# First layer two pairs ahead of the second instead of one, in an audio tower on one Trainium2 core

## The reference, cut to what matters

```
h = tok(x)                                    # batch norm over all 64 x 252 positions
h = h + softmax_attention(layernorm(h))       # layer 0: 8 heads of 16, band of 0.1 in the scores
h = h + moe(layernorm(h))                     # 8 experts, hidden 256, exact gelu, top 2
h = h + linear_attention(layernorm(h))        # layer 1: elu features, cumulative sums, 8 x 64 values
h = h + causal_ffn(layernorm(h))              # 2 causal heads of 64, then 8 experts, hidden 512, tanh gelu
```

## Time and profile before

| | us |
|---|---|
| median of three runs | 3990.13 |
| lowest, highest | 3986.05, 3990.76 |
| the profiled execution, its own time | 3990.81 |
| its span in the profile | 3989.1 |
| TensorE busy | 3827.6 |
| VectorE busy | 3155.2 |
| ScalarE busy | 2855.2 |
| GpSimd busy | 2782.1 |

### The profile page before, as it was taken

How to read it: one execution, slowest core, us unless ns; L and a number is a source line. 1 busy time by engine, 2 the same in 40 slices (tenths; PEclk the granted TensorE clock), 3 DMA queues, 4 the chain that set the end, 5 groups by cost and what they waited for, 6 DMA issues and landing times.

```text
span 3989.1 us, 105187 instructions
## 1 busy us (share of the span) xinstructions
PE 3827.6 (96%) x41541; PEld 2742.8 (69%) x41541; DVE 3155.2 (79%) x8623; ACT 2855.2 (72%) x4958; POOL 2782.1 (70%) x2725
## 2 busy tenths in 40 slices
PE   9899999999999999999999999999999999999988
PEld 4356767777667777776777777677777767777766
DVE  4367888887888778888878788878878887888876
ACT  4257777777777777777777777777777777777764
POOL 2156777777767777776777777777777677777766
PEclk9999999999999999999999999999999999999999
DMA  6111110011111001111000111100111110011100
GB/s 181 55 30 30 33 33 17 22 30 30 33 33 32 18 20 33 30 33 33 26 24 20 30 33 33 33 17 23 29 30 33 33 33 18 20 33 30 30 17 7
DMA packets 137277, 127.71 MB, mean 32 GB/s; under 512 B 29008, under 2 KB 135568, under 8 KB 136784
## 3 DMA queue, kind: packets, MB, share of 16 engines
q1 hardware_dynamic: 136784, 120.97, 10.5%
HBM read 71.12 MB, written 49.55 MB: 30 GB/s over the span
## 4 chain that ended last, share of the span: by engine, by line
PE 71%; DVE 16%; ACT 6%; POOL 3%; issue 2%; DMA 1%; SPq 1%; ACTq 0%; DVEq 0%
PE pf L1358 12%; PE pf L1360 11%; PE pf L1359 11%; PE pa L1653 5%; DVE h L1342 4%; PE pa L1358 4%; PE pa L1359 4%; PE pa L1360 4%; PE pa L1503 3%; PE pa L1635 3%; DVE hid_hi L1328 3%; PE pa L1489 2%; ACT hid L935 2%; PE pa L1404 2%; PE pa L1465 2%
## 5 line engine op out<-in xcount | busy, mean ns | idle before, releaser
L724 POOL TENSOR_TENSOR hid_lo<-hid,hid_hi 128x504 f16<-128x504 f32 x1536 | 1805.5, 1192 | 822.5 <-DVE hid_hi L1328 822.5
L935 ACT ACTIVATE hid<-pf,vec 128x504 f32<-128x504 f32 x1536 | 1021.1, 680 | 447.9 <-PE pf L1360 407.2
L1358 PE MATMUL pf<-w_hi,hid_hi 128*126 128x128 f16 x6144 | 1127.4, 224 | 88.0 <-DVE h L1342 79.0
L1360 PE MATMUL pf<-w_hi,hid_lo 128*126 128x128 f16 x6144 | 1108.7, 221 | 0.0
L1359 PE MATMUL pf<-w_lo,hid_hi 128*126 128x128 f16 x6144 | 1108.5, 221 | 0.0
L1358 PEld LDWEIGHTS pf<-w_hi,hid_hi 128*126 128x126 f16 x6144 | 843.4, 137 | 239.5 <-DVE h L1342 161.2
L1359 PEld LDWEIGHTS pf<-w_lo,hid_hi 128*126 128x126 f16 x6144 | 845.1, 138 | 14.0 <-issue 0.2
L1360 PEld LDWEIGHTS pf<-w_hi,hid_lo 128*126 128x126 f16 x6144 | 846.8, 138 | 0.0
L1328 DVE CAST hid_hi<-hid 128x504 f16<-128x504 f32 x1536 | 765.6, 521 | 95.7 <-ACT hid L935 89.4
L1342 DVE SCALAR_TENSOR_TENSOR h<-pf,gates,h 126x128 f32<-126x128 f32 x2048 | 573.5, 342 | 144.7 <-PE pf L1360 141.7
L1358 PE MATMUL pf<-xf_hi,w_hi 128*128 128x504 f16 x1536 | 578.7, 377 | 16.9 <-ACT hid L935 16.1
(11 more groups left out here) (239 smaller groups left out, 7731.5 us busy)
## 6 DMA issues: line engine op xcount, KB each, us to landing
qk_spread<-terms SPq DMA_DIRECT2D x224, 126.0 KB, 2.6
qk_spread<-terms SPq DMA_DIRECT2D x192, 63.0 KB, 2.3
y_scratch<-hid SPq DMA_DIRECT2D x32, 252.0 KB, 2.1
y_in<-y_scratch SPq DMA_DIRECT2D x32, 252.0 KB, 3.1
terms<-qk_hi SPq DMA_DIRECT2D x32, 252.0 KB, 2.4
terms<-qk_lo SPq DMA_DIRECT2D x32, 252.0 KB, 2.5
qk_spread<-terms SPq DMA_DIRECT2D x32, 252.0 KB
terms<-ot_hi SPq DMA_DIRECT2D x32, 252.0 KB, 2.4
```

The source lines that it names most:

```text
L724: nc.gpsimd.tensor_tensor(hid_lo[:, c % 8], hid[:, c % HIDS], hid_hi[:, c % 8], ALU.subtract).then_inc(hid_lo_done[c % 2], 1)
L935: nc.scalar.activation(hid[:, c % HIDS], pf[:, c % 2, 0:TOK], func, bias=vec[:, bias:bias + 1]).then_inc(F["hid_ready"], 1)
L1358: nc.tensor.matmul(out, ah, bh, start=start, stop=False, skip_group_check=skip)
L1360: return nc.tensor.matmul(out, al, bh, start=False, stop=stop, skip_group_check=skip)
```

## The change

The first layer's attention and experts now run two pairs ahead of the second layer instead of one (`AHEAD = 2`). The tile `h0` becomes a ring of two. START does the first layer of pairs 0, 1 and 2 and the queries of four pairs; there are 29 middle rounds instead of 30, in which round r has the queries of pair r + 3, the first layer of pair r + 2, the second attention of pair r; END has the second attention and experts of pairs 30 and 31. The strings of all engines are new. The space of the ring comes partly from `bn_part`, which now lies in `ha`.

```
+AHEAD = 2
 def before_first(p):
     if not isinstance(p, Count):
-        return p, max(p - 1, 0)
-    return p, p - 1
+        return p, max(p - AHEAD, 0)
+    return p, p - AHEAD
 def before_second(p):
     if not isinstance(p, Count):
-        return min(p + 2, PAIRS), p
-    return p + 2, p
+        return min(p + AHEAD + 1, PAIRS), p
+    return p + AHEAD + 1, p
...
-    for r in range(1, last):
-        parts = {"a": first_attention(r + 1), "l": second_attention(r),
-                 "h": up(chunks_of(1, r - 1)[LAG:] + chunks_of(0, r + 1) + chunks_of(1, r)[:LAG]),
-                 "o": down(chunks_of(1, r - 1) + chunks_of(0, r + 1))}
-        if r + 2 < PAIRS:
-            parts["q"] = queries_and_keys(r + 2)
+    for r in range(1, PAIRS - AHEAD):
+        parts = {"a": first_attention(r + AHEAD), "l": second_attention(r),
+                 "h": up(chunks_of(1, r - 1)[LAG:] + chunks_of(0, r + AHEAD) + chunks_of(1, r)[:LAG]),
+                 "o": down(chunks_of(1, r - 1) + chunks_of(0, r + AHEAD))}
+        if r + AHEAD + 1 < PAIRS:
+            parts["q"] = queries_and_keys(r + AHEAD + 1)
         in_order(middle, parts)
...
-        bn_part = sb("bn_part", [128, PAIRS * 6])
-        h0 = sb("h0", [128, TILES, D])
+        h0_all = sb("h0", [128, AHEAD, TILES, D])
+        bn_part = ha[:].rearrange("p t d -> p (t d)")[:, 0:PAIRS * 6]
+        def h0(p):
+            return h0_all[:, p % AHEAD]
...
-                dve.wait_ge(S1["carried"], n(p))
-                dve.wait_ge(S1["xn_ready"], n(p * 2 - 1))
-                add_bias2(0, p, ha, h0)
+                dve.wait_ge(S1["carried"], n(p - AHEAD + 1))
+                dve.wait_ge(S1["xn_ready"], n((p - AHEAD) * 2 + 1))
+                add_bias2(0, p, ha, h0(p))
```

More of the change, by code:

```diff
@@ L203 @@
[L203 to L206, removed]
+SP_START = ("qqqqaqaqqqllllaqqqqqqqq")
+SP_ROUND = ("alllloqqqq")
+SP_END = ("llllolllloo")
@@ L256, in run_rounds @@
     start, middle, end = orders
-    last = PAIRS - 1
+    ahead = range(AHEAD + 1)
     in_order(start, {
         "w": unused or repeat(None),
-        "q": chain(queries_and_keys(0), queries_and_keys(1), queries_and_keys(2)),
-        "a": chain(first_attention(0), first_attention(1)), "l": second_attention(0),
-        "h": up(chunks_of(0, 0) + chunks_of(0, 1) + chunks_of(1, 0)[:LAG]),
-        "o": down(chunks_of(0, 0) + chunks_of(0, 1))})
-    for r in range(1, last):
-        parts = {"a": first_attention(r + 1), "l": second_attention(r),
-                 "h": up(chunks_of(1, r - 1)[LAG:] + chunks_of(0, r + 1) + chunks_of(1, r)[:LAG]),
-                 "o": down(chunks_of(1, r - 1) + chunks_of(0, r + 1))}
-        if r + 2 < PAIRS:
-            parts["q"] = queries_and_keys(r + 2)
+        "q": chain(*(queries_and_keys(p) for p in range(AHEAD + 2))),
+        "a": chain(*(first_attention(p) for p in ahead)), "l": second_attention(0),
+        "h": up([c for p in ahead for c in chunks_of(0, p)] + chunks_of(1, 0)[:LAG]),
+        "o": down([c for p in ahead for c in chunks_of(0, p)])})
+    for r in range(1, PAIRS - AHEAD):
[4 more added lines that the diff above has]
+            parts["q"] = queries_and_keys(r + AHEAD + 1)
         in_order(middle, parts)
+    left = range(PAIRS - AHEAD, PAIRS)
     in_order(end, {
-        "l": second_attention(last), "h": up(chunks_of(1, last - 1)[LAG:] + chunks_of(1, last)),
-        "o": down(chunks_of(1, last - 1) + chunks_of(1, last))})
+        "l": chain(*(second_attention(p) for p in left)),
+        "h": up(chunks_of(1, left[0] - 1)[LAG:] + [c for p in left for c in chunks_of(1, p)]),
+        "o": down(chunks_of(1, left[0] - 1) + [c for p in left for c in chunks_of(1, p)])})
 def program(nc, x_dram, w_dram, vec_dram, row_dram, b2_dram, out_dram):
@@ L991, in _ @@
             dve.wait_ge(T["y_stats"], n(PAIRS))
-            nc.vector.bn_aggr(bn[:], bn_part[:]).then_inc(bn_step, 1)
+            nc.vector.bn_aggr(bn[:], bn_part).then_inc(bn_step, 1)
             dve.wait_ge(bn_step, 3)
@@ L1185, in linear_and_causal_attention @@
                 dve.wait_ge(F["gated"], n(first + EXPERTS))
[L1186 removed]
+                norm_stats(1, h0(p))
                 yield
@@ L1332, in output @@
                 experts_before, before = chunks_before(kind, p)
-                h = h_of[kind]
+                h = h2 if kind else h0(p)
                 per = (CHUNKS0, CHUNKS1)[kind]
```

60 lines of the change are left out of this document (33 added, 27 removed).

## The result

| | us |
|---|---|
| before, median of three runs | 3990.13 |
| after, median (lowest, highest) | 4024.53 (4019.37, 4025.45) |
| ratio, with its 95% interval | 1.0085 [1.0066, 1.0103] |
| the profiled execution of after, its own time | 4019.37 |
| its span | 4017.7 |

The change makes the kernel slower, by 34 us in the medians and by 28.6 us between the profiled executions (4019.37 - 3990.81). The rest of this document explains the 28.6.

A forecast was written before the change was run, and what follows sets the result against it. The prediction held that TensorE's order sets the time, through edges bound by chains and short waits inside rounds. It summed 3990.8 + 32.2 (edges) - 18.6 (middle orders) - 0.7 (median) to 4003.7, rounded to 4004 us, range 3964 to 4040.

The forecast's parts named there:

- The likeliest case: Middle rounds: a gain of 0.3 to 1.1 us each, total 3990 to 4014 us; chance 0.36.
- One round fewer: Middle rounds: dropping one removes 117.2 us, its work going into START and END.
- START, +58.4 predicted: START: third pair's queries, attention and experts take 104.6 us where 46.2 followed before, +58.4 us (about +45 to +66).
- END, +91 predicted: END: a second second-layer attention that can't overlap the first adds 91 us (83 to 96).
- Edges +32.2 predicted: START and END together, less one middle round: +32.2 us (+11 to +45).
- cheaper edges: Rival on START and END: they add only +45 and +83 us, total 3983 us; chance 0.07.
- The 18 dummies: START: 18 more dummy products fill waits of the chain and cost nothing; uncovered, under 6.8 us.
- The ring, the counts, `bn_part`: Ring of `h0`, wait counts, statistics placed in `ha`: no instruction added, no effect on either side.
- The new middle orders: 29 middle rounds: rearranged waits sum to -0.64 us a round, -18.6 us in all (-3.4 to +1.0 a round).
- A long cast ahead of an eviction: Rival on VectorE in middle rounds: a long cast on TensorE's way adds 0.95 us a round, total 4031; chance 0.11.
- The round doesn't change: Rival on middle rounds: same work in another sequence, no gain, total 4022 us; chance 0.14.
- Waits really go: Rival on middle rounds: only the DMA wait is new, a round gains 1.9 us, total 3967; chance 0.32.

The follow-up runs named there:

- experiment 1: Changed kernel (two pairs ahead, its START and END) with the middle-round orders of the kernel before on all engines; 4020.51 us, ratio 1.0084.
- experiment 4: Changed kernel without the 32 dummy products beside the third pair's first attention in START; 4028.87 us, ratio 1.0103.
- experiment 6: The rounds of experiment 5 run one pair ahead, with START and END of the kernel before; 4068.05 us, ratio 1.0201.
- experiment 10: The spliced round of experiment 9 run two pairs ahead, with START and END of the changed kernel; 4110.92 us, ratio 1.0306.
- Experiment 11: Changed kernel with, on VectorE, the eviction ahead of `o34` moved before the casts of `h32` and `h33`; 3998.89 us, ratio 1.0023.
- experiment 3: Changed kernel with the next pair's query and key projections, and ScalarE's and VectorE's steps for them, moved ahead of `o42`; 4097.23 us, ratio 1.0274.
- experiment 5: Changed kernel with the next pair's query and key projections slightly earlier (ahead of `o44`) and VectorE's query, key and value steps moved; 4095.77 us, ratio 1.0270.
- experiment 7: Kernel before with the next pair's query and key projections moved late, behind `o45`, as in the changed kernel; 4112.57 us, ratio 1.0310.
- experiment 9: One pair ahead, changed kernel's round orders, but from `o40` the old order on TensorE, VectorE and ScalarE; 4078.25 us, ratio 1.0222.
- experiment 2: Kernel before (one pair ahead, old START and END) with the changed kernel's middle-round orders on all engines; 3993.11 us, ratio 1.0018.

## Why the prediction was right, and where it was off

The prediction was 4004 us, in a range of 3964 to 4040, with "slower" as the likeliest; measured were 4024.5, and the profiled execution took 15 us more than the 4004.4 of the sum. The direction was right by the mechanism: the edges cost what was forecast. The likeliest case itself, a gain of 0.3 to 1.1 us a round and 3990 to 4014 us, did not come; the number is inside the range because the range was wide enough for a round that gains nothing (4022). Going through the steps:

- **One round fewer, -117.2:** right; experiment 1 has rounds of the old length.
- **START, +58.4 predicted, +56.4 measured,** closer than its parts, since two misses partly cancel. "The same chain" up to the second pair's first attention was 5.8 us shorter than before (149.7 us after the stage's start against 155.5), which the prediction did not have. What follows took 108.4 us where 104.6 were forecast: 5.6 to the third pair's transposes (taken as 4), 27.3 from there to its first scores (taken as 24), the attention chain 51.5 (51.1), the experts 24.1 (25.5). I did not look into the 5.8; the stretches show 2.6 of it in the first attention of pair 0 (68.2 against 70.8) and 3.5 in its experts (23.1 against 26.6).
- **END, +91 predicted, +90.6 measured,** again with two misses that cancel. The first second-layer attention ends at 3882.52 and the next at 3976.65, 94.1 us apart (taken as 91), of which the chain itself takes 87.5 (88.5 before). The part up to the first one's end was 2.0 us shorter than before (92.4 against 94.4) and the rest behind the last one's end 1.5 (41.1 against 42.6). The rows show the last product of pair 30's chain, the first transposes of pair 31's, and its last product.

```profile
3882.52 0.44 PE L1440 MATMUL pa<-b_terms,gate_t 128*126 128x128 f16 x4 [0.80 <-ACT gate_t L809]
...
3889.14 0.65 PE L1417 MATMUL pa<-ident,xn 126*128 126x126 f32 x4 [0.66 <-ACT xn L799]
...
3976.65 0.39 PE L1440 MATMUL pa<-b_terms,gate_t 128*126 128x128 f16 x4
```

- **Edges +32.2 predicted.** 56.4 + 90.6 - 117.2 = 29.8 in the profiles; 27.7 to 32.7 in three pairs of runs. The rival *cheaper edges* is refuted.
- **The 18 dummies at nothing:** nothing speaks against it. It is not the whole of it: experiment 4, with 32 others, shows that such products can pay.
- **The ring, the counts, `bn_part` at nothing:** nothing speaks against it; experiments 1, 6 and 10 leave no remainder for them.
- **The new middle orders, -0.64 us a round predicted, -0.08 measured** over all rounds (117.21 against 117.29; +0.03 in steady state, and the last round 3.2 us shorter). This is the term that was mis-sized: -18.6 us predicted and -2.3 measured, so 16 us too much gain. With the edges 2.4 lower and the token stage 1.1 longer, 4004.4 becomes 4019. Its parts, as the mean time lost a round:

| part | before | after | difference | predicted |
|---|---|---|---|---|
| `o36`, and the new wait at `o34` | 2.01 | 0.53 + 1.61 | +0.13 | -0.04 |
| `o38`, `o40` | 0.53 + 0.35 | 0 | -0.88 | -0.9 |
| `h30`, and the new wait at `o28` | 0.66 | 0.48 | -0.18 | 0 |
| the second layer's `l38`, now behind a hidden chunk | 0.33 | 0 | -0.33 | -0.3 |
| the round's first scores | 0.14 | 0.99 | +0.85 | +0.7 |
| `h37`, `h39`, behind ScalarE's exps | 0 | 0 | 0 | +0.2 |
| `l35`, behind `o20` | 0 | 0.37 | +0.37 | not foreseen |
| all the rest, with the changes between f32 and f16 steps | | | -0.04 | -0.3 |

  - The largest miss is a wait that the prediction did not have: `l35` waits for VectorE's low half of its input (the `xt_lo` row above, 0.2 us idle, 0.37 lost). The next is the gain from fewer changes between f32 and f16 steps, for which no row had a price: next to nothing of it came. The 0.2 for `h37` and `h39` and the 0.2 saved at `h30` were missed the other way.
  - *A long cast ahead of an eviction* was priced as a rival at 0.95 us a round on top. A long cast does stand ahead of the eviction that `o34` waits for (1.26 us against 0.41), so I followed VectorE's queue with too short a cast there. (Even so the row's idle time, 1.16, is the 1.15 that was forecast: something else in that reckoning was off the other way, and I don't know what.) But the old order had one too, at `o36` (1.36), and the two waits together grew by 0.13 us only: the long cast moved with the wait and did not come on top. Experiment 11 shows that the order at this place is worth 0.9 us a round; that it is the cast's length is argued, not shown. The Trainium skill (GPSIMD Engine Reference, 1. Specifications) names contention of GpSimd with VectorE instructions in a 2-port mode or with two SBUF inputs; by that rule the traces agree, with the numbers in the last section, though no row tells in which mode the cast runs.
  - The first scores: the mean was nearly right, but I had taken a DMA's arrival as fixed, and it varies. In two rounds 3.4 us at half clock followed.
  - The saved table load is real (six at the gelu's line in a round instead of seven) and brought no time: ScalarE wasn't what TensorE waited for.
- **The round doesn't change** (3rd case, 4022 us) comes closest in the number: 4019.4 profiled. Its reason, that the change does the same in another sequence, is not what happened: TensorE lost about 4.2 us a round less at the old places (`o36`, `o38`, `h30`, `o40`, `l38`, and 0.29 at `a29`) and about as much more at the new ones. That the two sides came out equal is chance as far as the runs show.
- **Waits really go** (3967 us) needed a round 1.9 us shorter. Experiment 11 got half of it (117.2 to 116.2) with one move, so the rival named something that exists; the change's order did not reach it.

**Not settled:** whether a round could have both the early keys and the short border. Experiments 3, 5, 7 and 9 each moved the keys with neighbours, and each made a round 2.5 to 4.3 us longer: by new waits at the border, and in experiments 5 and 7 also by the granted clock. The token stage's 1.1 us is no part of the change: over the fourteen profiled executions that stage takes 131.4 to 133.0 us, whichever kernel it is.

## What to carry to other kernels

Price the depth of a software pipeline by its edges first: each pair further ahead costs a first layer alone in START and a second layer alone in END less one round, here 30 us, and that price was nearly the same with three different rounds. The round itself gains from depth only where its order uses it; the rounds here took nearly the same time at either depth (before and experiment 1, experiment 2 and after, 5 and 6, 9 and 10). When you move a step ahead of another in a queue that TensorE waits for, take each duration at the length that it has beside its new neighbours, not at its median. And when single rounds stand out, look at the granted clock before you blame the wait alone.

## What the runs showed of the hardware

- **The 128x504 cast on VectorE beside GpSimd.** In the trace of before the 384 casts that no GpSimd instruction overlaps take 0.41 to 0.42 us each. Of the 395 that began while GpSimd's subtraction L724 ran, all but one ended 0.28 us after it, or took 0.41 us where that is longer; the longest took 1.38. These 395 average 737 ns, the other 1141 average 446. Not every GpSimd instruction does this: the 183 casts that began under L647 (126x4) and not near its end took 0.41 us too.
- **A DMA's landing has scatter of its own.** SyncE starts the store of the keys' low halves 1.56 us before each round's first step in the changed kernel (rounds 2 to 28, within 0.01 us), and it lands 2.3 to 4.2 us later. With the same instructions in every round, rounds that have the spread keys on TensorE's path differ by 1.6 us (116.4 to 118.0) even without those that have a stretch at half clock. Where the keys are off the path the stores scatter as much (2.2 to 3.8 us in before) and the rounds repeat: 117.2 in before, 120.0 in experiment 3 and 120.3 in experiments 9 and 10.
- **The granted clock falls inside a middle round, too.** For 3.4 us at a time it stood at half, in 2 rounds of 29 in after (119.5 us on average, the others but the last 117.1), in 12 of 29 in experiment 5 and in 21 of 30 in experiment 7; in before in one of 30, with 117.7 instead of 117.2 us. The page's 40 slices don't show it.
- **Products that nobody reads pay beside a chain that leaves TensorE idle.** The same chain took 51.5 us at a granted clock of 0.97 in its stretch, and 56.2 us at 0.92 without them.
